# Scan stage of a fused token mixer: projections split 128 + 64, steps reordered, and three of sixteen products with C moved from VectorE to GpSimd

## The chip, the cores and the metric

The kernel runs on one core of a Trainium2 chip. The metric is the device time of one execution in microseconds; three runs of the kernel before gave 1500.68, 1502.33 and 1514.03, median 1502.33. TensorE is PE in the rows, VectorE is DVE, ScalarE is ACT, GpSimd is POOL, the engine that issues most DMAs is SP.

## The reference

Three layers follow each other on 32 sequences of 82 tokens (1 class token, 49 patches, 32 text tokens) of width 192: a convolutional tokenizer, a selective scan (Mamba) block with its gated feed-forward part, and attention with a mixture of experts. The change is in the second one:

```python
h = rmsnorm(x, w_norm1)
z = h @ W_in.T
z = z * sigmoid(h @ W_gate.T)
dt_in, Bm, Cm = split(einsum('bld,kd->blk', z, W_xproj), [96, 112])
dt = softplus(einsum('blr,dr->bld', dt_in, W_dt) + b_dt)
A_bar = exp(dt[..., None] * A)              # A = -exp(A_log), 16 states
Bx = (dt * z)[..., None] * Bm[:, :, None, :]
h_t = A_bar_t * h_(t-1) + Bx_t              # along the tokens
y = einsum('blds,bls->bld', h, Cm) + D_skip * z
x = residual + y @ W_out.T
hf = rmsnorm(x, w_ffn_norm)
out = x + (silu(hf @ W_gate_ffn.T) * (hf @ W_up.T)) @ W_down.T
```

Inner width is 384, the feed-forward width 512. All of it is float32; only the rows of C that TensorE spreads are split into three bfloat16 parts.

## The kernel before

The scan block works in 8 rounds of 4 sequences. N = 328 is the number of tokens of a round, and 384 channels lie on 128 partitions as three blocks, so a full tile of a round is 128x984. The function `mamba` writes each engine's program by hand. A round has 16 steps, one per state s, and `program` (L767) sets for each engine what stands in a step: `step` (the scan of the round i), `post` (output projection and feed-forward of round i-1) and `pre` (norm, z, x-projection, softplus of round i+1). VectorE and GpSimd take `step` first; TensorE and ScalarE take `post` and `pre` first (`side_first`). Round 0 has no post, round 7 no pre.

In a step of the scan:
- GpSimd makes Bx for state s+3 (`inputs`, L1339) from dtz and the rows of B, which SP has spread over 128 partitions through DRAM (Bb).
- ScalarE makes the decays A_bar for state s+2 into two PSUM banks, one per half (`decays`, L1092); each half waits until the scan has read the half before it.
- VectorE multiplies the scanned states hs with C (L1239; called a product here) and then scans the next state in two halves (L1229).
- TensorE spreads the row of C of state s+2 over 128 partitions (L941, `sel`), into one of two banks, waiting for the product that read that bank; then it adds hs times C to y in PSUM by a product with the identity (L956, called y0 to y15 here). After state 15 VectorE drains y (L1195).

Around it, by step: 1 and 2 hold the output projection O in two halves (L905) and the residual adds (L1205), 2 the turn (transpose) of hn (L858), 3 to 5 the three pairs z and gate (L878), each followed by tanh on ScalarE and the z product on VectorE (L1174), 6 the x-projection X (L886), 7 the turn of hf, 8 and 9 the step sizes (L864), 10 to 13 the four pairs of the feed-forward part (L921) with tanh and the av products (L1210, L1213), 14 and 15 the down projection N in two halves (L933). The side work shares two PSUM banks in the order of `SIDE_TILES`; `free` waits until the tile two places before has been read. Softplus is Relu, Abs, Exp (u), two copies that round 1+u (`ax`, L1056 and L1058), Ln (L1060), and four 128x984 operations on GpSimd that end in dt and dtz. The width 192 is contracted as 96 + 96, so a pair of projections is 4 matmuls, and each float32 matmul is 2 passes in the rows.

## Time and profile before

| | us |
|---|---|
| runs | 1500.68, 1502.33, 1514.03 |
| profiled execution | 1509.22 |
| its span | 1507.4 |
| TensorE, VectorE, ScalarE, GpSimd busy in the span | 1240.3, 1035.6, 707.5, 753.8 |
| granted TensorE clock, mean | 0.901 |
| scan rounds 0 to 7 (to the drain of y) | 305 to 833 |

The profiled execution is one run with the hardware profiler on; its rows are in microseconds from the span's start. In a timeline a row stands for instructions of one line that follow each other (x is their number), and the bracket tells how long the engine stood idle before it and what released it. In the windows the last three numbers are the granted clock of TensorE (1.00 is full speed), the DMA share and GB/s.

### The profile page before, as it was taken

To read this page: it belongs to the slowest core of one execution; us is meant where nothing else is said; L and a number is where in the kernel's file an instruction comes from. 1 tells how busy PE (TensorE), PEld (TensorE's weight loads), DVE (VectorE), ACT (ScalarE), POOL (GpSimd) and SP (SyncE) were. 2 spreads that over 40 slices of the span, in tenths; PEclk is the share of its full clock that TensorE was granted. 3 is DMA by queue.
4 is the path that set the end of the run, shared out by engine and by line. 5 is a ranking of instruction groups with operands and counts; after the bars stand their busy time and mean duration, and the time that the engine had idled before them with its cause. 6 is when DMAs were issued, how large, how long until landed. Compare 5 with 4: busy or idle time off the path is not lost. (4 is left out here: it accounts for less than half of the span.)

```text
span 1507.4 us, 19621 instructions
## 1 busy us (share of the span) xinstructions
PE 1240.3 (82%) x5818; PEld 819.3 (54%) x5819; DVE 1035.6 (69%) x1960; ACT 707.5 (47%) x1486; POOL 753.8 (50%) x492
## 2 busy tenths in 40 slices
PE   6796635486989999899987899999996169999996
PEld 4342323242555555555553678877775147777775
DVE  3699787889989899989899556777784313333332
ACT  1137622467868686767765255554531022222221
POOL 2028974378677776858578301144445602222222
PEclk9697657689999999999999899999995579999999
DMA  5100000232404040322310001112211112222221
GB/s 164 54 1 0 28 9 28 99 114 94 135 1 135 0 134 13 121 68 66 131 32 1 1 34 51 45 55 69 61 49 30 37 48 38 35 35 35 38 35 22
DMA packets 71129, 80.89 MB, mean 54 GB/s; under 512 B 13230, under 2 KB 62917, under 8 KB 70969
## 3 DMA queue, kind: packets, MB, share of 16 engines
q1 hardware_dynamic: 51778, 68.50, 14.5%
q0 software_dynamic: 17152, 9.24, 4.5%
q10 hardware_dynamic: 2136, 2.37, 0.6%
q8 instruction: 32, 0.52, 0.2%
q14 instruction: 31, 0.25, 0.1%
HBM read 48.74 MB, written 30.01 MB: 52 GB/s over the span
## 5 line engine op out<-in xcount | busy, mean ns | idle before, releaser
L1346 POOL TENSOR_TENSOR Bx<-dtz,Bb 128x984 f32<-128x984 f32 x128 | 289.1, 2280 | 37.5 <-DVE hs L1229 37.5
L1229 DVE TENSOR_TENSOR_SCAN hs<-ps,Bx 128x492 f32<-128x492 f32 x256 | 287.8, 1165 | 23.2 <-POOL Bx L1346 14.9
L956 PE MATMUL ps<-hs,b_id 128*128 128x492 f32 x512 | 241.0, 593 | 11.9 <-DVE y L1195 9.5
L1100 ACT ACTIVATE ps<-dt,A 128x324 f32<-128x324 f32 (+1 forms) x512 | 212.1, 454 | 78.0 <-DVE hs L1229 77.8
L2070 POOL DMA_INDIRECT out<-yt,dest x48 | 74.2, 1547 | 221.4 <-DVE yt L2057 216.0
L1239 DVE TENSOR_TENSOR hs<-hs,ps 128x984 f32<-128x984 f32 x128 | 150.2, 1173 | 1.9
L1951 PE MATMUL e_ps<-W,xT 97*128 (+1 forms) x384 | 139.2, 505 | 1.6 <-ACT xT L2005 1.0
L956 PEld LDWEIGHTS ps<-hs,b_id 128*128 128x128 f32 x512 | 92.8, 194 | 86.4 <-issue 80.5
L2043 DVE COPY hT__9520<-e_ps 128x768 f32<-128x768 f32 x48 | 46.0, 958 | 131.3 <-PE e_ps L1960 130.9
L1970 PE MATMUL e_ps<-W,hT__9520 128*128 x576 | 109.2, 327 | 0.8 <-DVE yb L2051 0.8
L1846 POOL DMA_INDIRECT buckets<-XS,c_slot x64 | 90.6, 1416 | 37.7 <-DVE c_slot L1808 20.9
L2011 ACT ACTIVATE hb<-e_ps 128x768 f32<-128x768 f32 x48 | 38.9, 811 | 144.9 <-PE e_ps L1951 144.9
L1951 PEld LDWEIGHTS e_ps<-W,xT 97*128 97x128 f32 (+1 forms) x384 | 70.3, 193 | 55.5 <-issue 17.9
L1853 POOL TENSOR_TENSOR c_x<-c_x,bro 82x192 f32<-82x192 f32 x32 | 19.2, 600 | 157.2 <-DVE c_x L1702 157.1
L1970 PEld LDWEIGHTS e_ps<-W,hT__9520 128*128 128x128 f32 x576 | 91.4, 190 | 1.4 <-issue 1.4
L492 POOL TENSOR_TENSOR DF<-DF,prod 96x441 f32<-96x441 f32 x84 | 87.5, 1041 | 6.6
L921 PE MATMUL ps<-hfT,wug 96*128 96x328 f32 x256 | 80.5, 460 | 12.2 <-DVE av L1213 11.5
L1660 DVE TENSOR_REDUCE mx<-ps 82x12 f32<-82x984 f32 x32 | 37.6, 1176 | 59.4 <-PE ps L1565 59.4
L2005 ACT ACTIVATE xT<-e_ps,vec 96x128 f32<-96x128 f32 x96 | 38.5, 451 | 83.8 <-PE e_ps L1941 83.8
L941 PE MATMUL ps<-P,sel 96*128 96x328 bf16 x128 | 39.8, 312 | 45.5 <-DVE hs L1239 32.3
L921 PEld LDWEIGHTS ps<-hfT,wug 96*128 96x128 f32 x256 | 48.3, 196 | 49.8 <-DVE av L1213 27.4
L1578 PEld LDWEIGHTS ps<-V,PT 82*82 82x82 f32 x768 | 65.0, 161 | 11.0 <-issue 4.7
(251 smaller groups left out, 2415.7 us busy)
## 6 DMA issues: line engine op xcount, KB each, us to landing
Bb<-b_rows SPq DMA_DIRECT2D x32, 656.0 KB, 7.0
buckets<-b_zero SPq DMA_DIRECT2D x8, 2288.0 KB, 15.3
xg<-buckets SPq DMA_DIRECT2D x48, 104.0 KB, 1.9
xc<-in_xcol SPq DMA_DIRECT2D x4, 1176.0 KB, 9.2
W<-in_w1d SPq DMA_DIRECT2D x8, 582.0 KB
W<-in_w2d SPq DMA_DIRECT2D x8, 576.0 KB
out<-H SPq DMA_DIRECT2D x8, 246.0 KB
H<-P SPq DMA_DIRECT2D x4, 294.0 KB
```

What stands on the lines that cost most here:

```text
L492: g.tensor_tensor(out, a, prod[:, (9 * n + t) % PRODUCTS], ALU.add).then_inc(s_sum, 1)
L921: mm = pe.matmul(ps[:, wide(name, p), 0:N], wug[:, k, w_, m * 128:(m + 1) * 128], hfT[:, k, :], start=k == 0, stop=k == 1)
L956: mm = pe.matmul(ps[:, BANK_Y + h, 0:HALF], ident[:], f2(hs[:, s % LONG])[:, h * HALF:(h + 1) * HALF], start=s == 0, stop=s == STATE - 1)
L1100: a = act.activation(ps[:, BANK_A + h, c:c + w].rearrange("p (g t) -> p g t", t=S)[:, :, 1:S], dt[:, (par + t // STATE) % 2, m, g0 * S:g1 ...
L1229: v.tensor_tensor_scan(f2(hs[:, t % LONG])[:, c], ps[:, BANK_A + h, 0:HALF], f2(Bx[:, t % RING])[:, c], 0.0, ALU.mult, ALU.add).then_inc(s ...
L1239: v.tensor_tensor(hs[:, s % LONG], hs[:, s % LONG], ps[:, BANK_C + s % 2, 0:N].rearrange("p (a n) -> p a n", a=1).broadcast_to([128, NI, N ...
L1346: g.tensor_tensor(Bx[:, t % RING], dtz[:, p], Bb[:, p, t % STATE, :].rearrange("p (a n) -> p a n", a=1).broadcast_to([128, NI, N]), ALU.mu ...
L1578: mm = pe.matmul(ps[0:S, HEAD_OUT + c % 2, h * (DH + 1):(h + 1) * (DH + 1)], PT[:, c % 2, h, :], V[:, vpar, c, h, :], start=True, stop=True)
L1846: g.indirect_dma_start(out=xs, out_offset=bass.IndirectOffsetOnAxis(ap=slot[:, par, k, c:c + 1], axis=0), in_=XS[:, par, c, :], in_offset= ...
L1951: mm = pe.matmul(ps[:, 1 + 2 * p + h, 0:384], xT[c_, p, k, :], W1[c_, k, bass.ds(e, 1), h * 384:(h + 1) * 384].rearrange("p a n -> p (a n) ...
L1970: mm = pe.matmul(ps[:, 7, 0:D], hT[:, p, k, :], W2[:, k, bass.ds(e, 1), :].rearrange("p a n -> p (a n)"), start=k == 0, stop=k == KF - 1)
L2070: g.indirect_dma_start(out=out, out_offset=bass.IndirectOffsetOnAxis(ap=dest[:, p:p + 1], axis=0), in_=yt[:, p, :], in_offset=None, comput ...
```

## The change

Three things change in `mamba`, and nothing outside it but the layout of its weights.

1. The product with C of states 1, 3 and 5 (`POOLED`) is made by GpSimd from rows of C in SBUF (`Cb`), which SP spreads in one more DMA per round, behind the four of Bb. TensorE spreads 13 rows instead of 16, and adds y of a pooled state together with the next one.
2. The width 192 is contracted as 128 + 64. Of a pair, the two matmuls with 128 rows come first; the two with 64 rows read the lower half of the partitions for one bank and the upper half for the other. The turned hn and hf take 128 partitions, and ScalarE keeps them in three pieces instead of two.
3. The order: O, its residual adds and N are not spread over two steps any more; `dtin` is kept a step later; 1+u is rounded by one two-step operation on GpSimd (on VectorE in the first round) instead of two copies on ScalarE; Ln stands ahead of the second tanh; the relu goes to dt itself; GpSimd waits for u ahead of its Bx 13.

The core of the diff (N is joined in step 14 as O is in step 1, and the residual adds likewise):

```diff
+        POOLED = (1, 3, 5)
+        SPREAD = [s for s in range(STATE) if s not in POOLED]
+        NP_, NS_ = len(POOLED), len(SPREAD)
...
+                sp.wait_ge(s_cst, 2)
+                if j > 0:
+                    sp.wait_ge(s_hp, j * NP_)
+                sp.dma_start(Cb[:], b_d[par, STATE + POOLED[0]:STATE + POOLED[-1] + 1:2, :].rearrange("(a s) n -> a s n", a=1)
+                             .broadcast_to([128, NP_, N])).then_inc(s_Cb, 16)
...
-                        mm = pe.transpose(ps[0:HD, bank(names[k]), q * S:(q + 1) * S], src[:, q, k * HD:(k + 1) * HD],
-                                          ident[0:S, 0:S])
+                        mm = pe.transpose(ps[:, bank(names[k]), q * S:(q + 1) * S], src[:, q, k * 64:k * 64 + 128], ident[0:S, 0:S])
                     mm.then_inc(done, 1)
+
+            def pair(banks, w, x, m, done):
+                c_ = slice(m * 128, (m + 1) * 128)
+                for k in range(2):
+                    pe.matmul(ps[:, banks[k], 0:N], w[:, k, c_], x[:, 0, :], start=True, stop=False)
+                for k in range(2):
+                    half = slice(64 * k, 64 * k + 64)
+                    pe.matmul(ps[:, banks[k], 0:N], w[half, 2, c_], x[half, 1, :], start=False, stop=True).then_inc(done[k], 1)
...
-                    for w_, name, done in ((1, f"RG{m}", s_gt), (0, f"RI{m}", s_zi)):
-                        free(name, j, other)
-                        for k in range(2):
-                            mm = pe.matmul(ps[:, bank(name), 0:N], wzg[:, k, w_, m * 128:(m + 1) * 128], hT[:, k, :],
-                                           start=k == 0, stop=k == 1)
-                        mm.then_inc(done, 1)
+                    free(f"RI{m}", j, other)
+                    pair((bank(f"RG{m}"), bank(f"RI{m}")), wzg, hT, m, (s_gt, s_zi))
...
+                if s == 1:
+                    pe.wait_ge(s_y, p + 1)
+                    for h in range(2):
+                        free(f"O{h}", p, other)
+                        for q in range(2):
+                            c = (2 * h + q) * S
+                            for k in range(NI):
+                                mm = pe.matmul(ps[0:S, bank(f"O{h}"), q * D:(q + 1) * D], y[:, k * N + c:k * N + c + S], wo[:, k, :],
+                                               start=k == 0, stop=k == NI - 1)
+                        mm.then_inc(s_o, 1)
...
-                    for w_, name, done in ((0, f"G{m}", s_g), (1, f"U{m}", s_up)):
+                    if not is_last(p):
+                        free(f"G{m}", p, other)
+                    elif m >= 2:
+                        pe.wait_ge(s_av, p * 4 + (m - 1))
+                    pair((wide(f"G{m}", p), wide(f"U{m}", p)), wug, hfT, m, (s_g, s_up))
...
+            def spread_c(i, par, n):
+                at_least(pe, s_hc, i * NS_ + n - 1)
+                if n % NS_ == 0:
+                    pe.wait_ge(s_P3, i + n // NS_ + 1)
+                pe.matmul(ps[:, BANK_C + (par * NS_ + n) % 2, 0:N], sel[:, SPREAD[n % NS_], :], P3[:, (par + n // NS_) % 2, :],
...
-                if not last or s + 2 < STATE:
-                    spread_c(i, par, s + 2)
+                if s in POOLED:
+                    return
+                n = SPREAD.index(s)
+                if not last or n + 2 < NS_:
+                    spread_c(i, par, n + 2)
+                if s - 1 in POOLED:
+                    add_y(i, s - 1)
                 add_y(i, s)
...
+            def keep_turned(dst, names, v_, done, kept, j):
+                high = slice(64, 128)
+                act.wait_ge(done, j * 2 + 1)
+                act.activation(dst[:, 0, :], ps[:, bank(names[0]), 0:N], ACT.Identity, bias=0.0, scale=vec[:, v_:v_ + 1]).then_inc(kept, 1)
+                act.wait_ge(done, j * 2 + 2)
+                for rows in (high, slice(0, 64)):
+                    a = act.activation(dst[rows, 1, :], ps[high, bank(names[1]), 0:N], ACT.Identity, bias=0.0, scale=vec[high, v_ + 1:v_ + 2])
+                a.then_inc(kept, 1)
...
-                    act.wait_ge(s_u, j + 1)
-                    act.activation(f2(ax[:]), f2(u[:]), ACT.Copy, bias=1.0).then_inc(s_w1, 1)
-                    act.wait_ge(s_w1, j * 2 + 1)
-                    act.activation(f2(ax[:]), f2(ax[:]), ACT.Copy, bias=-1.0).then_inc(s_w1, 1)
-                if s == 11:
-                    act.activation(f2(lnw[:]), f2(u[:]), ACT.Ln, bias=1.0).then_inc(s_c1, 1)
+                if s == 11 and other is None:
+                    logarithm(j)
...
+                    if m == 1 and other is not None:
+                        logarithm(other)
...
+                if s not in POOLED:
+                    n = SPREAD.index(s)
+                    v.wait_ge(s_scan, 2 * (i * STATE + s) + 2)
+                    v.wait_ge(s_pc, i * NS_ + (n + 1))
+                    v.tensor_tensor(hs[:, s % LONG], hs[:, s % LONG],
+                                    ps[:, BANK_C + (par * NS_ + n) % 2, 0:N].rearrange("p (a n) -> p a n", a=1).broadcast_to([128, NI, N]),
+                                    ALU.mult).then_inc(s_hc, 1)
...
-                    g.wait_ge(s_w1, j * 2 + 2)
+                    g.tensor_scalar(f2(ax[:]), f2(u[:]), 1.0, -1.0, ALU.add, ALU.add).then_inc(s_w1, 1)
+                    g.wait_ge(s_w1, j + 1)
                     g.tensor_tensor(f2(ax[:]), f2(u[:]), f2(ax[:]), ALU.subtract).then_inc(s_sp, 1)
                     g.wait_ge(s_sp, j * 2 + 1)
-                    g.tensor_tensor(f2(ax[:]), f2(ax[:]), f2(rl[:]), ALU.add).then_inc(s_sp, 1)
+                    g.tensor_tensor(f2(ax[:]), f2(ax[:]), f2(dt[:, par]), ALU.add).then_inc(s_sp, 1)
...
+            def times_c(i, s):
+                c = POOLED.index(s)
+                if c == 0:
+                    g.wait_ge(s_Cb, i * 16 + 16)
+                g.wait_ge(s_scan, 2 * (i * STATE + s) + 2)
+                g.tensor_tensor(hs[:, s % LONG], hs[:, s % LONG],
+                                Cb[:, c, :].rearrange("p (a n) -> p a n", a=1).broadcast_to([128, NI, N]), ALU.mult).then_inc(s_hp, 1)
+
             def step(i, par, s, last):
+                if s in POOLED:
+                    times_c(i, s)
+                if s == 10 and not last:
+                    g.wait_ge(s_u, i + 2)
```

How it moves the instructions, in a middle round. In the order's rows the register and semaphore instructions are left out. **TensorE**, steps 0 to 4, before (`hs,b_id` is a y, two matmuls each; `P_119,sel` a spread row of C):

```order
L956 MATMUL ps<-hs,b_id 128x492 x2
L905 MATMUL ps<-wo,y 82x192 x6
L941 MATMUL ps<-P_119,sel 128x328
L956 MATMUL ps<-hs,b_id 128x492 x2
L905 MATMUL ps<-wo,y 82x192 x6
L858 MATMUL ps<-b_id,hn 96x82 x4
L858 MATMUL ps<-b_id,hn 96x82 x4
L941 MATMUL ps<-P_119,sel 128x328
L956 MATMUL ps<-hs,b_id 128x492 x2
L878 MATMUL ps<-hT,wzg 128x328 x4
L941 MATMUL ps<-P_119,sel 128x328
L956 MATMUL ps<-hs,b_id 128x492 x2
```

and now:

```order
L968 MATMUL ps<-hs,b_id 128x492 x2
L919 MATMUL ps<-wo,y 82x192 x6
L919 MATMUL ps<-wo,y 82x192 x6
L870 MATMUL ps<-b_id,hn 128x82 x4
L870 MATMUL ps<-b_id,hn 128x82 x4
L950 MATMUL ps<-P_119,sel 128x328
L968 MATMUL ps<-hs,b_id 128x492 x4
L876 MATMUL ps<-hT,wzg 128x328 x2
L879 MATMUL ps<-hT,wzg 128x328 x2
L876 MATMUL ps<-hT,wzg 128x328 x2
L879 MATMUL ps<-hT,wzg 128x328 x2
L950 MATMUL ps<-P_119,sel 128x328
```

Both halves of O stand together, y1 has moved behind the turn to y2, and nothing stands between the first and the second pair.

**GpSimd**, steps 0 to 5 of the same round, now (before, the same rows without those of L1390):

```order
L1375 TENSOR_TENSOR Bx<-dtz,Bb 128x984
L1390 TENSOR_TENSOR hs<-hs,Cb 128x984
L1375 TENSOR_TENSOR Bx<-dtz,Bb 128x984
L1375 TENSOR_TENSOR Bx<-dtz,Bb 128x984
L1390 TENSOR_TENSOR hs<-hs,Cb 128x984
L1375 TENSOR_TENSOR Bx<-dtz,Bb 128x984
L1375 TENSOR_TENSOR Bx<-dtz,Bb 128x984
L1360 TENSOR_TENSOR b_rr<-b_ms,b_nh 82x4
L1390 TENSOR_TENSOR hs<-hs,Cb 128x984
L1375 TENSOR_TENSOR Bx<-dtz,Bb 128x984
```

Each of the three products stands ahead of the Bx of its step and waits for its own scan.

**ScalarE**, step 7, between two steps' decays, now (before, `dtin` stood ahead of the decays, and hfT was two rows of L1085):

```order
L1046 ACTIVATE dtin<-ps 96x328
L1026 ACTIVATE hfT<-ps,vec 128x328
L1029 ACTIVATE hfT<-ps,vec 64x328 x2
L1075 ACTIVATE P_119<-R 32x328
L1076 ACTIVATE Pm<-R 32x328
```

The queue up to the decays for state 9 has `dtin` and one eviction more.

## Rows read from the trace of the kernel before

**Rows 1.** The page's first part: busy us, share of the span, instructions.

```profile
PE 1240.3 (82%) x5818; PEld 819.3 (54%) x5819; DVE 1035.6 (69%) x1960; ACT 707.5 (47%) x1486; POOL 753.8 (50%) x492
```

**Rows 2.** Windows by round: stretch, length, busy PE, PEld, DVE, ACT, POOL, clock, DMA, GB/s.

```profile
502.30:570.90 68.60, 62.72 (x226) 36.56 (x226) 61.78 (x69) 48.20 (x114) 48.62 (x25) 0.98 0.24 74
570.90:637.90 67.00, 61.02 (x226) 35.89 (x226) 61.78 (x68) 48.41 (x115) 48.88 (x25) 1.00 0.24 75
...
775.20:833.40 58.20, 44.54 (x144) 22.57 (x145) 55.70 (x60) 29.58 (x75) 38.95 (x20) 1.00 0.00 1
```

**Rows 3.** VectorE timeline, round from 570.9: start, duration, line, operation [idle before].

```profile
569.73 1.17 DVE L1239 TENSOR_TENSOR hs<-hs,ps 128x984 f32<-128x984 f32 x1
...
581.71 0.52 DVE L1205 TENSOR_TENSOR x<-xl,ps 82x384 f32<-82x384 f32 x1
...
586.89 0.50 DVE L1174 SCALAR_TENSOR_TENSOR z<-sg,ps 128x328 f32<-128x328 f32 x1 [0.36 <-PE ps L878]
587.30 1.17 DVE L1239 TENSOR_TENSOR hs<-hs,ps 128x984 f32<-128x984 f32 x1
588.39 2.25 DVE L1229 TENSOR_TENSOR_SCAN hs<-ps,Bx 128x492 f32<-128x492 f32 x2
...
604.86 2.25 DVE L1229 TENSOR_TENSOR_SCAN hs<-ps,Bx 128x492 f32<-128x492 f32 x2
...
621.38 2.25 DVE L1229 TENSOR_TENSOR_SCAN hs<-ps,Bx 128x492 f32<-128x492 f32 x2 [1.33 <-POOL Bx L1346]
...
628.23 0.50 DVE L1213 SCALAR_TENSOR_TENSOR av<-th,ps 128x328 f32<-128x328 f32 x1
...
637.94 1.61 DVE L1195 SCALAR_TENSOR_TENSOR y<-z,vec,ps 128x328 f32<-128x328 f32 x4
```

**Rows 4.** TensorE timeline of the same round.

```profile
572.70 1.89 PE L956 MATMUL ps<-hs,b_id 128*128 128x492 f32 x4 [1.43 <-DVE y L1195]
574.42 2.11 PE L905 MATMUL ps<-wo,y 128*82 128x192 f32 x12
...
582.29 0.49 PE L858 MATMUL ps<-b_id,hn 82*96 82x82 f32 x4 [1.72 <-DVE x L1205]
...
584.40 2.37 PE L878 MATMUL ps<-hT,wzg 96*128 96x328 f32 x8
...
596.40 3.47 PE L886 MATMUL ps<-z,wx 128*96 128x328 f32 x12
...
628.87 2.80 PE L933 MATMUL ps<-wdn,av 128*82 128x192 f32 x16
```

**Rows 5.** ScalarE timeline of the same round.

```profile
601.99 0.95 ACT L1085 ACTIVATE hfT<-ps,vec 96x328 f32<-96x328 f32 x2
...
612.38 1.01 ACT L1056 ACTIVATE ax<-u 128x984 f32<-128x984 f32 x1
...
616.71 1.28 ACT L1060 ACT_TABLE_LOAD   x1
618.00 1.02 ACT L1060 ACTIVATE lnw<-u 128x984 f32<-128x984 f32 x1
```

**Rows 6.** Windows around the fall of the clock, round from 502.3.

```profile
512.00:514.00 2.00, 0.37 (x5) 0.37 (x6) 2.00 (x4) 0.48 (x1) 0.79 (x1) 1.00 0.00 0
514.00:516.00 2.00, 2.00 (x6) 1.03 (x4) 1.05 (x2) 1.84 (x5) 1.48 (x1) 0.51 0.00 0
```

**Rows 7.** TensorE timeline in the tokenizer: 128-row passes, then 128 and 64 rows.

```profile
99.90 12.02 PE L230 MATMUL ps<-xc,wc 128*128 128x392 f32 x36
...
113.33 0.90 PE L254 MATMUL ps<-D,pwm 128*96 128x392 f32 x2
114.16 0.90 PE L256 MATMUL ps<-D,pwm 64*96 64x392 f32 x2
```

**Rows 8.** GpSimd's groups by shape: count, busy us, mean ns of one.

```profile
L1346 POOL TENSOR_TENSOR Bx<-dtz,Bb 128x984 f32<-128x984 f32 x128 | 289.1, 2280 | 37.5 <-DVE hs L1229 37.5
...
L495 POOL MEMSET PF<- 96x4132 f32 x3 | 10.5, 3539 | 0.1
```

More of the change, by code:

```diff
@@ L79 @@
 V_ROW = 120
-V_N = 121
+V_H_NORM = 121
+V_HF_NORM = 123
+V_N = 125
 CH = 4
@@ L896, in post @@
             def post(p, par, s, other):
-                if s in (1, 2):
-                    h = s - 1
-                    if h == 0:
-                        pe.wait_ge(s_y, p + 1)
-                    free(f"O{h}", p, other)
-                    for q in range(2):
-                        c = (2 * h + q) * S
-                        for k in range(NI):
-                            mm = pe.matmul(ps[0:S, bank(f"O{h}"), q * D:(q + 1) * D], y[:, k * N + c:k * N + c + S], wo[:, k, :],
-                                           start=k == 0, stop=k == NI - 1)
-                    mm.then_inc(s_o, 1)
+                if s == 1:
[8 more added lines that the diff above has]
+                        mm.then_inc(s_o, 1)
                 if s == 7:
@@ L924, in post @@
-                if s in (14, 15):
-                    h = s - 14
-                    if h == 0:
-                        pe.wait_ge(s_av, p * 4 + 4)
-                    if not is_last(p):
-                        free(f"N{h}", p, other)
-                    for q in range(2):
-                        c = (2 * h + q) * S
-                        for k in range(NF):
-                            mm = pe.matmul(ps[0:S, wide(f"N{h}", p), q * D:(q + 1) * D], av[:, k, c:c + S], wdn[:, k, :],
-                                           start=k == 0, stop=k == NF - 1)
-                    mm.then_inc(s_dn, 1)
@@ new lines, in post @@
+                if s == 14:
+                    pe.wait_ge(s_av, p * 4 + 4)
+                    for h in range(2):
+                        if not is_last(p):
+                            free(f"N{h}", p, other)
+                        for q in range(2):
+                            c = (2 * h + q) * S
+                            for k in range(NF):
+                                mm = pe.matmul(ps[0:S, wide(f"N{h}", p), q * D:(q + 1) * D], av[:, k, c:c + S], wdn[:, k, :],
+                                               start=k == 0, stop=k == NF - 1)
+                        mm.then_inc(s_dn, 1)
@@ L978, in ending @@
                 post(last, 1, 1, None)
-                post(last, 1, 2, None)
                 fr.turn(pe)
@@ L1277, in ending @@
                 post(last, 1, 1, None)
-                post(last, 1, 2, None)
                 v.wait_ge(fr.s_r1, 1)
@@ L2082, in _halves, with _two_thirds, _paired @@
     return out
+def _two_thirds(a):
+    import numpy as np
+    a = np.asarray(a).reshape(192)
+    return np.stack([a[0:128], np.concatenate([a[128:192], a[128:192]])], axis=1)
+def _paired(first, second):
+    import numpy as np
+    first, second = np.asarray(first).T, np.asarray(second).T
+    return np.stack([first[0:128], second[0:128], np.concatenate([first[128:192], second[128:192]])], axis=1)
 def _mixed(loc, g):
```

109 lines of the change are left out of this document (50 added, 59 removed).

## The prediction

> **What bounds the kernel now.** The page's totals come first [rows 1]: TensorE 82%, VectorE 69%, GpSimd 50% busy. These are means over stages, so the next view is the windows cut by round of the scan [rows 2]. In a middle round (570.9 to 637.9) TensorE is busy 61.0 us of 67.0, VectorE 61.8, GpSimd 48.9, ScalarE 48.4: two engines are nearly full, the other two have 18 us each. The window 502.3 to 570.9 does the same work in 68.6 us, at a clock of 0.98 instead of 1.00. Four of the six middle rounds are of this kind (68.6 to 68.8 us), two take 67.0. The last round (775.2 on) takes 58.1 and gives TensorE only 44.5 us of work: there VectorE alone sets the pace.
>
> The VectorE timeline of the 67 us round [rows 3] shows two scan halves (2.25 us) and a product with C (1.17; the scan behind it starts after 1.09, 587.30 to 588.39) per state, and where it stands still: 0.36 before the first z, 1.33 before the scan of state 13. The TensorE timeline [rows 4] shows why: after the projections O it waits 1.72 for VectorE's second residual add, and from there to the turn of hf it never stops. So neither engine bounds the round by itself; the chain passes from one to the other, and only what lies on it counts.
>
> **The products on GpSimd.** Three of 16 products per round leave VectorE: 3 x 1.09 = 3.3 us. GpSimd gets them at the price of the Bx row of the same shape, 2.28 us [rows 8], so 6.8 us, and for `ax<-u` a one-source operation of 984 elements: the memset gives a floor of 0.86 ns per element, 0.85 us, the Bx row a ceiling of 2.28. 48.9 + 6.8 + 0.9 to 2.3 = 56.6 to 58.0 us, still under 67. That Bx costs 1.94 times VectorE's product says that the move only pays if GpSimd's time is idle time. The Trainium skill ("GPSIMD Engine Reference", Engine selection) says to keep elementwise work on VectorE, GpSimd being about twice as slow for two inputs. Obeyed, the rule would leave the products where they are; the trace agrees on the price.
>
> **Does the 3.3 us reach the end? A walk through one middle round**, 0 being the start of product 0 (569.73), with durations of rows 3 to 5:
> - Before: second residual add at 12.0 (581.71), first z/gate pair at 14.7 (584.40), z0 at 17.2, projection X at 26.7 (596.40), turn of hf 31.8, scan 9 at 35.1 (604.86), scan 13 at 51.7 (621.38), last av product over at 58.9, next drain at 68.2 (637.94).
> - Now scan 2 follows scan 1 without a product: 5.0 to 7.3. Its decays are just in time (half of the bank is free 1.1 us before, and ScalarE takes 0.85). Then both residual adds stand in one place: y0 from 3.0, O twice 1.95, over at 8.6, so VectorE waits 0.9 us for the second half and does product 2 at 9.1 to 10.2. Of 1.1 saved, 0.9 has become a wait.
> - TensorE stands behind product 2 (C for state 6 first), then adds y1 and y2 together (3.3): pair 0 at 13.75 instead of 14.7, z0 at 16.1 instead of 17.2.
> - Pair 1 needs the bank that z0 frees. Before, y3 covered that wait; now nothing does: TensorE waits 0.6. Pair 1 to 18.8, y3 and y4 to 22.3, pair 2 to 24.5, z2 at 24.6 instead of 25.2.
> - X needs z2, and y5 no longer covers it: X 25.1 to 28.4 (1.6 earlier), but then y5 and y6 stand ahead of the turn of hf: 31.85. Before: 31.8. TensorE's work up to here is the same, so **all of VectorE's 3.3 us has gone into waiting for TensorE**.
> - ScalarE now evicts hf's turn in three pieces instead of two (+0.43) ahead of the decays for scan 9 [rows 5]: scan 9 at 35.5, 0.4 late.
> - Both `ax` copies leave ScalarE (2 x 1.02) and Ln moves ahead of the second tanh. Ln's two table loads and itself (1.28 + 1.02 + 1.28) stay between the decays of states 12 and 13, so VectorE now waits about 0.9 for that tanh where it waited 1.33 for the decays: the 0.4 comes back, scan 13 at 51.7.
> - From the last av product TensorE does N0, N1, y14, y15 in place of N0, y14, N1, y15: the same 9.1 us (628.87 to 637.94). Next drain: 68.2.
>
> Net for a round at full clock: **0 us**, and I allow 1 us either way. GpSimd keeps up: its third product ends near 22.7, Bx 8 at 25 (wanted at 30). The new wait for u ahead of Bx 13 holds Bx 13, the softplus and dtz; by the walk Bx 15 is ready at 58.3 to 59.7 and wanted at 60.1; the two slacks are 5 and at least 0.4. On SP, the rows of C (504 KB) come after the four Bb groups and are used some 35 us later: 0.
>
> **The split 128 + 64.** A pair was 8 passes in 2.21 us, 0.277 each. It stays 8 passes, of which 4 use half the rows. The nearest rows are the tokenizer's [rows 7]: 36 passes of 392 columns with 128 rows take 0.334 each, and where 128 and 64 rows alternate every two passes, 0.415 each. That is 0.16 us per change of height, and a pair has two: +0.33. Against it, two adjacent matmuls on different halves of the array and in different banks may overlap. No row here shows such a pair; between none and both passes that is 0 to -0.55. In the timelines matmuls start in program order, and each is two passes, so only the second pass of the one can lie beside the first of the other: one pass, -0.28. The pair stays at 2.21 + 0.33 - 0.28 = 2.26 (ends 1.98 and 2.54; where drains cost nothing, 1.66). The Trainium skill ("TensorEngine Tiling (Array Packing)", Key Properties) says both that changing the mode drains the array and that tiles run in parallel. By the second alone a pair would take six passes, 1.66; the trace shows the first.
>
> **The clock.** In the 68.6 us rounds the granted clock falls from 1.00 to 0.51, the lower level of 1.2 GHz, right after the 1.72 us pause before the second half of the turn of hn [rows 6, 4], and y2 and the pair behind it run at half speed: 1.6 to 1.8 us a round. By the walk that pause shrinks to 0.2 + 0.7, with 0.6 more at pair 1. I take the drops as gone: **-6.8 us**.
>
> **The other stretches.** Last round: no z, no Ln, TensorE has 14 us to spare, so VectorE's 3.3 less the 0.9 wait come through: **-2.4**. First round: no residual adds, but the same walk (y1 and y2 behind product 2, pair 2 behind y3 and y4) turns the gain into a wait at z2 and leaves -0.3. Ahead of scan 0 VectorE gets one more operation of 984 elements (0 to 1.2, by the product's row), part of it under GpSimd's work: +0.5. After the last round four pairs and one eviction: +0.5. Softplus, table loads, transposes to 128 columns: 0, hidden as before.
>
> **Sum:** 0 - 6.8 - 2.4 - 0.3 + 0.5 + 0.5 = -8.5 on the profiled execution's 1509.2, so 1500.7. That execution is 6.9 us above the median of the three runs (1502.3); on the median: **1494 us**.
>
> **Rivals.**
> - *The clock drops stay* (20%). TensorE still pauses 1.4 us at the drain and several times under 1.1. Against it speaks that the round from 570.9 had the full 1.72 pause and clock 1.00: shorter pauses should bring fewer. Then 1494 + 7 = 1501.
> - *VectorE's time comes through* (20%). If the halves overlap more than I take, or y1 and y2 get out earlier than my walk has them, TensorE gives way at z2 and at hf, where all was lost. At the limit 8 x 3.3 = 26 and the clock's 6.8: 1469; half of it, 1480.
> - *Slower: the change of height, serial.* A pair at 2.54 adds 0.33 at each of seven pairs. Three lie ahead of scan 9 on TensorE's chain, those of states 12 and 13 behind av: about 1.6 to 2.3 a round, +10 to +14 over six, so 1504 to 1508 with the drops gone, 1515 with them. It is slower than before once a pair costs more than about 0.2 net. For it: rows 7; against: the overlap. 15%.
> - *GpSimd late.* The engine that is 1.94 times slower becomes the bound, at Bx 15, whose slack is 0.4 us with the dear one-source operation: 1 us late in six rounds is +6, 1500. For: two new waits in its queue. Against: 9 us idle a round. 5%. The Trainium skill ("GPSIMD Engine Reference", Engine selection) speaks for this one.
> - That the change doesn't move the work is excluded: the order of instructions shows it.
>
> Forecast 40%. **Range 1478 to 1511**: it takes in half of the fast rival, the drops and most of the slow one. The likeliest case's own is 1488 to 1500. Within 1% is 1487 to 1517, about what a measurement can tell. Faster by over 1%: the fast rival and a tenth of the rest, 0.28. Slower by over 1%: the worst of the serial case, 0.08. Within: 0.64.
>
> **What would show it.** Middle rounds all near 67 us, drain to drain, at clock 1.00 (the higher level, 2.4 GHz); VectorE about 58 us busy in each, with new waits at the second residual add (0.9), at z2 (about 2, on TensorE) and before scan 9 (about 2, on ScalarE); the last round near 55.7; pairs near 2.25 us; GpSimd at 57. Wrong, if z2 comes before 24, if pairs leave 2.0 to 2.5, if the clock still drops after the drain, or if scan 15 waits for Bx.

## The result, and the profile after

The changed kernel takes **1528.94 us** (median of 20 runs, 1515.53 to 1536.08), the kernel before 1509.23 (20 runs). The ratio is 1.0116, 95% interval 1.0086 to 1.0146: slower by 1.2%. The forecast was 1494 us, within 1478 to 1511: the kernel was to get faster, and it got slower.

First the page's busy line after (us, share, instructions), to be held against [rows 1]:

```profile
PE 1239.5 (81%) x5794; PEld 798.0 (52%) x5795; DVE 1010.5 (66%) x1938; ACT 700.7 (46%) x1486; POOL 830.7 (54%) x523
```

VectorE has 25 us less, as it should after 24 products. The span went from 1507.4 to 1532.3 all the same. The windows of the changed kernel, cut from drain to drain (length, busy PE, PEld, DVE, ACT, POOL, clock, DMA, GB/s), say where:

```profile
303.90:371.30 67.40, 47.12 (x127) 20.65 (x127) 55.38 (x53) 43.83 (x99) 60.47 (x28) 0.88 0.36 115
371.30:439.60 68.30, 59.87 (x223) 32.02 (x223) 58.18 (x66) 47.83 (x115) 59.29 (x29) 1.00 0.25 83
439.60:509.50 69.90, 60.01 (x224) 32.09 (x224) 58.42 (x66) 48.91 (x116) 60.39 (x29) 1.00 0.25 81
509.50:579.60 70.10, 61.11 (x222) 32.67 (x222) 58.39 (x66) 46.48 (x111) 57.39 (x28) 0.98 0.24 80
...
787.80:846.00 58.20, 44.37 (x140) 21.02 (x141) 52.44 (x57) 29.35 (x76) 47.70 (x24) 0.97 0.08 20
```

Against [rows 2]: a middle round at full clock takes 68.3 us, not 67.0, though VectorE is busy 3.4 us less in it. The first round went from 61.7 to 67.4. The last one gained nothing (58.2). From scan 0 to the last drain the kernel before takes 528.5 us, the changed one 542.2: +13.7, and +13.3 in a second profile of it. Behind the last drain its first profile has 12.2 us more than before. These 12.2 us can't be laid to the change: the second profile of the same kernel has 670.0 us there where the first has 686.3, and before had 674.1. The two windows below are the same 50 us of the span, inside that later stage, in the first profile and in the second (where the stage begins 2.9 us later); the clock is the number behind the busy times:

```profile
1062.60:1112.60 50.00, 47.53 (x343) 39.33 (x343) 30.69 (x95) 21.33 (x40) 22.50 (x19) 0.86 0.21 58
```

```profile
1062.60:1112.60 50.00, 46.71 (x386) 38.91 (x385) 35.67 (x113) 25.18 (x46) 22.83 (x19) 1.00 0.22 62
```

So the loop is read apart from the total below. The medians of 20 runs differ by 19.7 us and the loops of the two profiles by 13.3 to 13.7, so some 6 us of the slowdown lie outside the loop, and no profile here says where. Now one quiet middle round on VectorE (start, duration, line, operation, idle before and its releaser), as in [rows 3]; product 0 is at 438.52:

```profile
438.52 1.17 DVE L1267 TENSOR_TENSOR hs<-hs,ps 128x984 f32<-128x984 f32 x1
...
447.18 0.55 DVE L1231 TENSOR_TENSOR x<-xl,ps 82x384 f32<-82x384 f32 x1 [1.09 <-PE ps L919]
447.65 1.17 DVE L1267 TENSOR_TENSOR hs<-hs,ps 128x984 f32<-128x984 f32 x1
...
454.86 0.50 DVE L1200 SCALAR_TENSOR_TENSOR z<-sg,ps 128x328 f32<-128x328 f32 x1 [1.61 <-ACT sg L1065]
...
463.44 0.49 DVE L1200 SCALAR_TENSOR_TENSOR z<-sg,ps 128x328 f32<-128x328 f32 x1 [2.25 <-ACT sg L1065]
...
474.92 1.18 DVE L1255 TENSOR_TENSOR_SCAN hs<-ps,Bx 128x492 f32<-128x492 f32 x1 [2.79 <-ACT ps L1126]
```

Product 1 took 1.09 us of VectorE's path, and the second residual add now waits 1.09. Then come 1.61 and 2.25 before z0 and z2, and 2.79 before scan 9, which starts 36.4 us into the round (35.1 before). TensorE's side of it, to be held against [rows 4]:

```profile
447.79 0.50 PE L870 MATMUL ps<-b_id,hn 82*128 82x82 f32 x4 [0.36 <-DVE x L1231]
448.88 0.31 PE L950 MATMUL ps<-P,sel 96*128 96x328 bf16 x1 [0.59 <-DVE hs L1267]
449.03 3.47 PE L968 MATMUL ps<-hs,b_id 128*128 128x492 f32 x8
452.33 1.27 PE L876 MATMUL ps<-hT,wzg 128*128 128x328 f32 x4
453.53 0.82 PE L879 MATMUL ps<-hT,wzg 64*128 64x328 f32 x4
455.41 1.37 PE L876 MATMUL ps<-hT,wzg 128*128 128x328 f32 x4 [1.06 <-DVE z L1200]
...
464.08 3.52 PE L901 MATMUL ps<-z,wx 128*96 128x328 f32 x12 [1.15 <-DVE z L1200]
```

y1 and y2 stand together (3.47 us, eight passes) between product 2 and pair 0; y3 and y4 stand so before pair 2. GpSimd's groups in the whole run (count, busy us, mean ns of one, idle before) have two new rows beside [rows 8]:

```profile
L1390 POOL TENSOR_TENSOR hs<-hs,Cb 128x984 f32<-128x984 f32 x24 | 54.5, 2269 | 29.2 <-DVE hs L1255 29.2
L1345 POOL TENSOR_SCALAR ax<-u 128x984 f32<-128x984 f32 x7 | 24.6, 3511 | 0.1
```

### The profile page after: what moved, and what is told of

It is laid out like the page before. It is cut to its first block and busy times, and to the rows that moved or that the text cites. A ratio compares the mean times of both kernels' runs of the same rounds, so it can differ in the third digit from the quotient of the medians.

```text
span 1532.3 us, 19580 instructions
## 1 busy us (share of the span) xinstructions
PE 1239.5 (81%) x5794; PEld 798.0 (52%) x5795; DVE 1010.5 (66%) x1938; ACT 700.7 (46%) x1486; POOL 830.7 (54%) x523
## 5 line engine op out<-in xcount | busy, mean ns | idle before, releaser
L1267 DVE TENSOR_TENSOR hs<-hs,ps 128x984 f32<-128x984 f32 x104 | 122.0, 1173 | 3.8 <-issue 0.9
L1701 DVE TENSOR_REDUCE mx<-ps 82x12 f32<-82x984 f32 x32 | 37.7, 1177 | 66.5 <-PE ps L1606 66.5
L950 PE MATMUL ps<-P,sel 96*128 96x328 bf16 x104 | 32.6, 315 | 55.4 <-DVE hs L1267 43.0
L1390 POOL TENSOR_TENSOR hs<-hs,Cb 128x984 f32<-128x984 f32 x24 | 54.5, 2269 | 29.2 <-DVE hs L1255 29.2
L1606 PE MATMUL ps<-kB,qT 128*82 128x328 f32 (+1 forms) x256 | 65.5, 404 | 3.1 <-DVE E L1705 2.0
## 6 DMA issues: line engine op xcount, KB each, us to landing
buckets<-b_zero SPq DMA_DIRECT2D x8, 2288.0 KB, 16.3
```

Source lines behind the costliest of these rows:

```text
L1267: v.tensor_tensor(hs[:, s % LONG], hs[:, s % LONG], ps[:, BANK_C + (par * NS_ + n) % 2, 0:N].rearrange("p (a n) -> p a n", a=1).broadcast_ ...
L1606: mm = pe.matmul(ps[0:S, SCORES + h0 // 6, (h0 % 6) * S:(h0 % 6 + h1 - h0) * S], qT[:, par, m_, q * S:(q + 1) * S], kB[:, par, m_, q, j:j ...
```

## The experiments

"Loop" is scan 0 to the last drain of the profile, "round" a middle round with full clock and no wait at the loop's end (one round alone in e2, e5, e13 and e16, two in e9, none in e3). Medians are over the runs of each kernel; ratios are to the kernel before on the same chip.

| kernel | median us | ratio (95%) | loop | round |
|---|---|---|---|---|
| before | 1509.2 | 1 | 528.5 | 67.0 |
| changed | 1528.9 | 1.0116 (1.0086 to 1.0146) | 542.2 | 68.3 |
| e1 no products on GpSimd | 1499.95 | 0.9935 (0.9899 to 0.9972) | 511.9 | 64.95 |
| e12 the same again | 1494.5 | 0.9903 (0.9870 to 0.9936) | 511.9 | 64.96 |
| e2 changed, copies on ScalarE | 1527.3 | 1.0141 (1.0089 to 1.0192) | 545.5 | 69.4 |
| e3 before + products only | 1537.7 | 1.0213 (1.0162 to 1.0264) | 555.3 | 71.0 at clock 0.98 |
| e4 changed, again | 1527.1 | 1.0126 (1.0086 to 1.0166) | 541.8 | 68.3 |
| e5 changed, y in turn | 1513.9 | 1.0011 (0.9969 to 1.0052) | 528.4 | 65.4 |
| e6 e1, y in pairs | 1522.9 | 1.0062 (1.0028 to 1.0096) | 538.4 | 68.3 |
| e7 before + order only | 1504.9 | 0.9955 (0.9922 to 0.9988) | 513.1 | 64.9 |
| e8 before + split only | 1517.6 | 1.0039 (0.9997 to 1.0081) | 530.3 | 67.7 |
| e9 products left out | 1491.7 | 0.9903 (0.9868 to 0.9939) | 513.4 | 64.7 |
| e10 e1, copies on ScalarE | 1499.2 | 0.9943 (0.9909 to 0.9976) | 519.9 | 65.9 |
| e11 before + projection in one step | 1490.1 | 0.9875 (0.9827 to 0.9923) | 512.0 | 65.0 |
| e13 e5, counts of 16 | 1511.2 | 0.9996 (0.9954 to 1.0039) | 528.0 | 65.4 |
| e14 e11 again | 1488.2 | 0.9864 (0.9828 to 0.9900) | 512.1 | 65.0 |
| e15 e11, both projections | 1494.7 | 0.9898 (0.9858 to 0.9937) | 511.8 | 65.0 |
| e16 e11 + products, y in turn | 1508.2 | 0.9993 (0.9960 to 1.0026) | 521.5 | 64.9 |

**e1: the change without its products.**

```
- POOLED = (1, 3, 5)
+ POOLED = ()
```

> The changed kernel without its second part: all 16 products with C are on VectorE again, the rows of C are not loaded; the split 128 + 64, the conversion on GpSimd and the order stay. Theory A (the new order and split on TensorE and ScalarE make scans 2, 9 and the residual additions late, whoever multiplies with C): the middle rounds keep 68.0 to 68.6 us (before 66.97, changed 68.35), round 0 gets shorter by 2 to 4, total 1520 to 1530, ratio to the kernel before 1.008 to 1.014. Theory B (GpSimd is too full, its conversion of 3.50 us and three products of 2.27 us make Bx 14 and 15 late): without the three products the waits for Bx go, the middle rounds fall to 67.0 to 67.4 and round 0 to 62 to 63, total 1508 to 1513, ratio 1.000 to 1.003.

The rounds fell below both expectations, to 64.95, each of the six alike and none with a fall of the clock. So the split and the order *gain* 16.6 us in the loop, and the products cost 30, together with the pairs of y: where no state is pooled, no addition is put off to the next step, so this run takes both away and doesn't tell them apart (e5 and e6 do). Neither theory had rounds below 67. Round 0 took 63.8. Such a round in e12's profile (the same kernel), on VectorE, its product 0 at 497.28:

```profile
497.28 1.17 DVE L1260 TENSOR_TENSOR hs<-hs,ps 128x984 f32<-128x984 f32 x1
...
505.44 1.06 DVE L1224 TENSOR_TENSOR x<-xl,ps 82x384 f32<-82x384 f32 x2
506.42 1.17 DVE L1260 TENSOR_TENSOR hs<-hs,ps 128x984 f32<-128x984 f32 x1
...
513.05 0.47 DVE L1193 SCALAR_TENSOR_TENSOR z<-sg,ps 128x328 f32<-128x328 f32 x1
...
520.34 0.47 DVE L1193 SCALAR_TENSOR_TENSOR z<-sg,ps 128x328 f32<-128x328 f32 x1
...
530.32 1.18 DVE L1248 TENSOR_TENSOR_SCAN hs<-ps,Bx 128x492 f32<-128x492 f32 x1 [1.42 <-ACT ps L1119]
```

and on TensorE:

```profile
505.89 1.81 PE L961 MATMUL ps<-hs,b_id 128*128 128x492 f32 x4
507.55 0.73 PE L863 MATMUL ps<-b_id,hn 82*128 82x82 f32 x8
...
509.91 1.27 PE L869 MATMUL ps<-hT,wzg 128*128 128x328 f32 x4
...
521.19 0.99 PE L894 MATMUL ps<-z,wx 128*96 128x328 f32 x3
```

Product 2 starts 9.14 us into the round here and 9.13 in the changed kernel: the product that was taken from VectorE brought it there no earlier. But y1 stands ahead of the turn of hn here, not behind product 2. Nor does TensorE stop once in this round between O and X. In the changed kernel's rows above it waits 0.36, 0.59, 1.06 and 1.15 us there, 3.2 us together, because y1, y3 and y5 no longer fill these places. Pair 0 comes at 12.6 (changed 13.8), z0 at 15.8 (16.3), z2 at 23.1 (24.9), X at 23.9 (25.6) and scan 9 at 33.0 (36.4). The last difference, 3.4, is that of the rounds.

**e2: the copies back on ScalarE.**

```
- g.tensor_scalar(ax, u, 1.0, -1.0, add, add)
+ act.activation(ax, u, Copy, bias=1.0); act.activation(ax, ax, Copy, bias=-1.0)
```

> The changed kernel with the sum and difference of 1 for the softplus made by ScalarE in two copies again, as before, not by one instruction of GpSimd (3.50 us) behind a wait for u ahead of Bx 13. Theory B (GpSimd late through that chain): round 0 falls from 67.4 to 63 to 64, each middle round loses the 0.4 + 0.95 us of waits for Bx (68.35 to 67.2), total 1510 to 1517. Theory A (order and split on TensorE and ScalarE): round 0 gains 3 to 4 us, the middle rounds stay at 68.0 to 68.9 since ScalarE gets two copies more behind which the tanh of the feed-forward gate stands, total 1523 to 1530.

For the middle rounds theory B falls: GpSimd has the 3.5 us less, and the rounds get longer (69.4, against 68.3). VectorE waits 1.81 for the tanh of the second feed-forward quarter where it waited 0.85. Theory A had this total (1527), but rounds of at most 68.9. Round 0 alone gained, 67.4 to 63.3, as both had it.

**e3: the products alone on the kernel before.**

> The kernel before with the second part of the change alone: GpSimd makes products 1, 3 and 5 from rows in SBUF; split 96 + 96, the two copies for the softplus on ScalarE and the order of the rest stay. Theory A: the products by themselves cost nothing; middle rounds 66.6 to 67.1, clock drops of 1.7 us in as many rounds or fewer, total 1500 to 1510, ratio 0.995 to 1.001. Theory B: GpSimd has 6.8 us more in a round, Bx 14 and 15 come 0.5 to 1.5 late and the middle rounds take 67.5 to 68.5, total 1513 to 1521. Third theory (VectorE's 3.3 us come through once the order is the old one): middle rounds 64.5 to 66, total 1490 to 1500.

Worst of all: 71.0 to 73.5 a round, each with a fall of the clock or a wait at the loop's end. The one at full clock takes 71.96 with such a wait of 2.71, so about 69.3 without it. The second residual add is one step later here than in the changed kernel, and in that round z0 waits 2.02, z2 2.48, scan 2 2.04. All three numbers expected were too low.

**e4: the changed kernel again.**

> The changed kernel once more, for a second profile of it. If the 12 us that lie behind the last round are caused by the change, that stretch is again 684 to 688 us; if they are the clock's luck of one execution, it is 672 to 680 with the loop 458 to 463 as before. If the waits of 1.4 us at the loop's branch (two of six rounds) belong to the kernel, they stand in the same rounds again.

Loop 541.8 (first profile 542.2), behind it 670.0 (686.3). The waits at the loop's end stand again in rounds 2 and 4, and the clock falls in rounds 1, 3 and 5. The stretch behind the loop differs by 16 us between two executions of one kernel; the 13.5 us of the loop are the change's.

**e5: y in turn.** `add_y(i, s)` for states 1, 3 and 5 at their own step:

```
  if s in POOLED:
+     add_y(i, s)
      return
...
- if s - 1 in POOLED:
-     add_y(i, s - 1)
```

> The changed kernel with one edit: TensorE adds states 1, 3 and 5 to y each at its own step (behind the output projection, behind pair 0, behind pair 2), not together with states 2, 4 and 6 behind VectorE's next product. In the changed kernel's round from 509.5 product 1 of GpSimd ends at 515.6 and product 3 at 524.9, while TensorE ends the projection at 518.7 and pair 0 at 526.0, so neither is waited for. Theory C (the pairs of additions, 3.5 us in one piece ahead of pairs 0, 2 and the X passes, cost the time): z0 comes 1.65 us earlier, the wait of pair 1 for z0 takes y 3, middle rounds fall from 68.3 (70 with the wait at the loop's end) by 3 to 4 us to 64.5 to 66.5, total 1498 to 1508. Theory D (GpSimd's own work is what costs, as it is slower by twice at the product and then late with Bx): rounds fall by less than 1 us, total 1518 to 1530.

Quiet rounds fall from 68.3 to 65.4, the loop by 13.8 us. The total lies at 1514, 6 above the expected range, since the waits at the loop's end and the clock drops stayed. Theory C holds for the rounds, D falls.

**e6: the same edit the other way.** In e1, with all products on VectorE:

```
+ if s in (1, 3, 5): return
+ if s in (2, 4, 6): add_y(i, s - 1)
  add_y(i, s)
```

> The kernel of the run without products on GpSimd (1499.95 us, rounds of 64.95) with one edit the other way: all 16 products on VectorE, but TensorE adds states 1 and 2, 3 and 4, 5 and 6 to y in pairs, behind product 2, 4 and 6, as in the changed kernel. Theory C: the round gets longer by most of what the changed kernel loses, 2 to 4 us (67 to 69), total 1512 to 1525. Theory D: 0 to 0.8 us a round, total 1498 to 1506. If VectorE being ahead is needed for the loss as well (it has 3.3 us less in the changed kernel), something between, with z0 late by 1.65 and no more.

64.95 becomes 68.32, the changed kernel's round, with GpSimd doing no product at all. VectorE's waits are those of the changed kernel:

```profile
458.51 0.50 DVE L1195 SCALAR_TENSOR_TENSOR z<-sg,ps 128x328 f32<-128x328 f32 x1 [0.49 <-ACT sg L1060]
467.10 0.49 DVE L1195 SCALAR_TENSOR_TENSOR z<-sg,ps 128x328 f32<-128x328 f32 x1 [1.20 <-ACT sg L1060]
478.57 1.18 DVE L1250 TENSOR_TENSOR_SCAN hs<-ps,Bx 128x492 f32<-128x492 f32 x1 [2.88 <-ACT ps L1121]
```

They are shorter at z0 and z2 by what VectorE itself now has to do, and nearly the same at scan 9 (2.88, 2.79). This pair of runs, e5 and e6, shows it from both sides: the placing of three additions on TensorE costs 2.9 us a round with GpSimd's products and 3.4 without them. Round 0 gets 4.7 us longer by it as well (68.5 against 63.8).

**e7 and e8: the order alone, the split alone, on the kernel before.**

> The kernel before with the order of the change alone (both halves of the output projection and of the residual additions in one step, both halves of the last projection in one step, the logarithm and the copy of dt_in later on ScalarE, the conversion on GpSimd), split 96 + 96, all products on VectorE. The two parts together brought the middle rounds from 66.97 or 68.65 to 64.95. If the order brings it: rounds of 65 to 66 and no clock drops, total 1500 to 1505. If the split brings it: rounds of 67 to 68.6, total 1507 to 1513.

> The kernel before with the split 128 + 64 alone, its order as before. The pair takes 2.02 us from start to end and not 2.21 + 0.33 twice over: three pairs in the first half of a round and four in the second make TensorE's part shorter by 0.5 each, 3.5 us a round. If the split brings the 2 us (and the end of the clock drops): rounds of 65 to 66, total 1500 to 1505. If the order brings it: 67 to 68.6, total 1506 to 1513. Evictions of the turned rows take 1.66 instead of 0.98 us, so a loss of up to 0.7 is possible too.

The order brings it all (64.9; the clock falls in one middle round, which takes 66.5, where it fell in four before). The split alone loses 0.7 a round (67.7): the turned rows leave in three evictions, the tanh waits for the whole pair, and VectorE waits 1.65 and 2.08 for decays behind them. Its 1518 us lie above both ranges. With the new order the same split costs nothing that the rounds show (64.95 against 64.9).

**e9: products left out.** Nobody multiplies states 1, 3 and 5.

> Leaves out part of the computation: nobody multiplies states 1, 3 and 5 with C (the output is not the reference's). Otherwise the kernel with y in turn, and no rows of C in SBUF, so VectorE is relieved of 3 x 1.09 us a round and GpSimd has nothing more to do. Theory E (in states 0 to 8 the chain from the drain over projection, residual additions, pairs and evictions on TensorE and ScalarE sets the pace, so VectorE's relief is worth nothing there): rounds of 64.5 to 65.4, as with all products on VectorE (64.95), total 1498 to 1508. If VectorE's time counted and GpSimd's slower product (2.27 us, rows of C, order behind Bx) ate it up: rounds of 62 to 63.5, total 1480 to 1492. The waits of 0.5 to 1.15 us without a releaser at the end of every second round: if they come from VectorE's shorter program they stand here too (total then 1501 to 1512), if from GpSimd's products they are gone.

Theory E holds for the rounds: 64.7, only 0.25 less than with all products on VectorE. The total, 1491.7, lies below its range, but e12 on the same chip has 1494.5 and the same ratio, 0.9903. One window of a quiet round, and, from another round, two of the waits that took the 3.3 us:

```profile
696.50:761.20 64.70, 59.22 (x223) 31.82 (x223) 58.33 (x67) 47.03 (x112) 52.24 (x26) 1.00 0.31 96
```

```profile
571.30 0.55 DVE L1223 TENSOR_TENSOR x<-xl,ps 82x384 f32<-82x384 f32 x1 [1.09 <-PE ps L912]
...
575.94 1.18 DVE L1247 TENSOR_TENSOR_SCAN hs<-ps,Bx 128x492 f32<-128x492 f32 x1 [0.83 <-ACT ps L1118]
```

VectorE waits for TensorE's projection, then for ScalarE's decays. Against e5 (65.4), GpSimd's slower products cost 0.7 a round. The waits at the loop's end stand here too, so they do not come from GpSimd's products.

**e10: e1 with the copies on ScalarE.**

> The kernel without products on GpSimd (1499.95 us) with the sum and difference of 1 again as two copies on ScalarE in place of one conversion on GpSimd of 3.50 us. If GpSimd's 3.5 us and its wait for u are what makes Bx 15 late by 1.1 us a round: the wait goes and rounds fall to 64.0 to 64.4, total 1492 to 1497. If ScalarE's two copies (1.9 us together, ahead of the first tanh of the feed-forward part) delay as much: 64.9 to 66.5, total 1499 to 1508.

The second: scan 15 no longer waits for Bx, but the tanh comes 2.21 late, and the round takes 65.9. Round 0 is the other way, 60.9 against 63.8, since there Bx 15 waits 3.3 us for the conversion. The conversion on GpSimd is worth 1 us a middle round and costs 2.9 in the first.

**e11 and e14: one piece of the order.** The kernel before with this alone, on TensorE and in the same way for the adds on VectorE:

```
- if s in (1, 2):
-     h = s - 1
+ if s == 1:
+     for h in range(2):
```

> The kernel before with one piece of the new order: both halves of the output projection in one step of TensorE and both residual additions in one step of VectorE. TensorE's 24 passes then stand in one piece and x1 is complete one step (about 3.9 us) earlier, and the turn of hn, pair 0 and z 0 stand as before. If this piece brings the order's 2 us: rounds of 65 to 66, total 1500 to 1506. If the last projection in one step, the later logarithm and dt_in and the conversion bring it: 66.6 to 68.6, total 1506 to 1512.

> The kernel before with both halves of the output projection and of the residual additions in one step, once more (four runs that count gave 1490.12 us, ratio 0.9875). Rounds of 65.0 again; expected 1490 to 1500 us and a ratio of 0.988 to 0.994, about that of the split and order together without products (0.9903 and 0.9935).

65.0 a round, loop 512.0 and 512.1: this piece is the order's whole gain. One middle round (66.7) still has a fall of the clock. The ratios are the lowest of all (0.9875 and 0.9864, the second just below what was expected), though their intervals overlap those of e9 and e12. Its TensorE rows, to be held against 572.70 to 582.29 of [rows 4], and the residual adds on VectorE:

```profile
566.38 4.06 PE L904 MATMUL ps<-wo,y 128*82 128x192 f32 x24
...
572.08 0.73 PE L858 MATMUL ps<-b_id,hn 82*96 82x82 f32 x8
```

```profile
569.97 1.06 DVE L1202 TENSOR_TENSOR x<-xl,ps 82x384 f32<-82x384 f32 x2
```

Both turns of hn run in one piece. The pause of 1.72 us between them is gone, and with it the pauses of 0.95, 0.36, 0.25 and 0.24 us that VectorE made in that part of the round before, 1.8 us of the 1.95.

**e12: e1 again.**

> The split and the order of the change with all products on VectorE once more, beside the run with the copies. The first time it took 1499.95 us, ratio 0.9935. Expected again 1498 to 1502 us, rounds of 64.95; if the first result was the chip's, the ratio lies above 0.998.

Loop 511.9 again. Its median is 4 us over e11's, which ran on the same chip, with an equal loop. The difference lies outside the loop, where single executions differ by up to 16 us, and I can't lay it to an edit.

**e13: counts of 16.**

```
- .then_inc(s_pc, 1)
+ .then_inc(s_pc, GAP[n % NS_])
```

`GAP` is 2 where a state is skipped, 1 elsewhere, so the count runs to 16 a round instead of 13; the count of VectorE's products (`s_hc`) is changed likewise.

> The kernel with y in turn (1513.88 us), with the semaphores of the C rows and of VectorE's products counting 16 a round in place of 13 (an increment of 2 where a state is skipped); no engine does other work. VectorE's loop body is then 263 instructions long, not 287 (269 in the kernel before). If the length of that body causes the 1.4 to 1.8 us of waits without a releaser at the end of rounds 2 and 4, they go and the ten further instruction transfers (41 against 31) with them, total 1509 to 1512. If the waits come from another thing in the kernels with 13 products, they stay, total 1513 to 1515.

The waits at the loop's end stand, although the total, 1511.2, falls into the range of the theory that they go:

```profile
504.53 1.18 DVE L1268 TENSOR_TENSOR hs<-hs,ps 128x984 f32<-128x984 f32 x1 [0.38 <-issue]
506.78 1.61 DVE L1223 SCALAR_TENSOR_TENSOR y<-z,vec,ps 128x328 f32<-128x328 f32 x4 [1.07 <-issue]
```

So do the 41 transfers on the instruction queue q14 (31 in every kernel with 16 products on VectorE, 41 or 42 in every one with 13). The lengths in the expectation leave out the instructions that only wait for a semaphore or signal one. With them the trace has 343 instructions of VectorE in two rounds (one pass of the loop's body) before, 331 in the changed kernel and 331 in e13. So this edit left the length as it was, and length is not excluded: every kernel with these waits has 331, every one without them 343, give or take a record. What the trace adds is where the ten further transfers lie. Six of them follow the two branches back to the loop's start, three behind each, of 8 KB. In the changed kernel the branch starts at 504.27 and VectorE's next instruction 2.86 us later, against 0.35 us before (500.60 to 500.95). The instruction queue in the changed kernel's window 504 to 511:

```profile
q14 instruction: 3, 0.02, 1.1%
```

The kernel before has none on that queue in 490 to 790. That the waits are waits for instructions is the likely reading; no run tests it, nor whether the length of the body or its place in VectorE's program brings the transfers on.

**e15: the last projection in one step too.**

> As the kernel with the output projection's halves in one step, and the 32 passes of the feed-forward's last projection in one step too. There VectorE waited 0.52 us a round for the second half of it: that wait goes, and the wait of 1.33 us for ScalarE or Bx at scan 14 or 15 takes some of it. Rounds of 64.5 to 65.0, total 0 to 4 us below the kernel with the first piece alone. A loss of up to 0.5 a round if y 14, now behind all 32 passes, makes the drain wait.

No gain: the rounds stay at 65.0, and the 0.52 before the second half becomes 0.67 before the drain.

**e16: the products on the best order.**

> Best case for the products on GpSimd: the kernel before with the output projection's halves in one step, products 1, 3 and 5 on GpSimd, y in turn, counts of 16. Theory E (the chain on TensorE and ScalarE sets the first half of a round): rounds of 65.0 to 65.8, not shorter than the 65.0 without products, and total 1497 to 1506. If the relief of VectorE is worth something on this order: rounds of 62 to 64.3, total 1480 to 1490.

The quiet round takes 64.9 against 65.0. The loop is 9.4 us longer by the waits at the loop's end, a single one up to 2.7 us here, and the clock drops behind them; the total, 1508, lies 2 above theory E's range.

## Why the prediction was wrong

**The walk through the round had the right places and too small waits.** It gave 9.1 for product 2 (measured 9.13), 13.75 for pair 0 (13.8), 16.1 for z0 (16.3), 24.6 for z2 (24.9), 25.1 for X (25.6), 31.85 for the turn of hf (32.4), 35.5 for scan 9 (36.4). The tanh came 0.85 behind, as said. Each small error has one sign. I let the gate's half of a pair end before the pair; in the rows both end together, so the tanh and z0 come later and pair 1 waits 1.06, not 0.6. The three evictions took 1.66 us where two took 0.98: +0.68, not +0.43. Scan 9 was 1.3 late, not 0.4: 0.6 from the turn of hf, 0.7 from the evictions.

**The step that failed is "the 0.4 comes back ... Net for a round at full clock: 0".** What is late at scan 9 does not come back: e1 to the changed kernel, scan 9 moves by 3.4 and the round by 3.4; before to changed, by 1.3 and 1.4. From scan 9 on VectorE is the pace, and a wait for the tanh only takes the place of a wait for the decays. Six rounds of 1.4 are 8 us. Two of the prediction's own signs of being wrong came with it: scan 15 waits for Bx (0.95), and the clock still falls behind the drain.

**"All of VectorE's 3.3 us has gone into waiting for TensorE" was right and half the truth.** e9 shows that the relief is worth 0.25 us on this order (e16 against e11: 0.1). But I set the time by comparing with the kernel before and so added two large effects to a nought without seeing either: the projection in one step gains 2 us a round (e11), the pairs of y lose 3 (e5, e6). I had written down both, "both residual adds stand in one place" and "adds y1 and y2 together (3.3)", and priced neither by itself.

**The first round** was to gain 0.3 and lost 4.4 to 5.7. Of it, 2.1 belong to the rest of the change (e1: 63.8 against 61.7). There Bx 15 comes 3.3 late behind the conversion, with no product on GpSimd. The remaining 2.3 to 3.6 come with the products and the pairs of y; the pairs by themselves add 4.7 (e6), the products without the pairs 2.0 (e5).

**The one-source operation** took 3.50 us, outside my bounds of 0.85 to 2.28. I had taken a memset for its floor and an operation with two inputs for its ceiling. GpSimd is busy 59.3, 60.4 and 57.4 us in the three middle rounds shown, not 57, and scan 15 waits 0.95 for Bx. In the middle rounds it is a miss of the size and not the cause of the loss: with the two copies on ScalarE in its place they got longer (e2 by 1.1, e10 by 1.0). In the first round it costs 2.9 (e10). The Trainium skill ("GPSIMD Engine Reference", Engine selection) calls work with one input on GpSimd "roughly line-rate"; this row disagrees, since VectorE did the same operation in 0.73 us.

**The split:** a pair takes 2.02 us from start to end (452.33 to the end at 454.35), of which four passes of 64 rows take 0.82. I had 2.26 with ends at 1.98 and 2.54, and before it was 2.21. The change of height and the overlap together come out 0.2 us shorter; what each is worth by itself no row tells (both at their best would be my 1.66). The rival of the serial pair falls all the same, as it needs 2.54. The kernel was slower by another mechanism.

**The clock, -6.8:** only half came. Two of the four drops went; two stayed, in rounds 3 and 5 (in e4's profile three, the third in round 1). Each stands behind a wait at the loop's end that I had no term for, 1.4 us in the changed kernel. The windows from 511 on show it (clock behind the busy times), at the lower of the two levels, 1.2 GHz:

```profile
511.00:513.00 2.00, 1.73 (x3) 0.95 (x4) 2.00 (x3) 0.74 (x2) 0.00 (x0) 0.69 0.00 0
513.00:515.00 2.00, 2.00 (x5) 0.94 (x4) 1.98 (x3) 1.43 (x4) 1.63 (x1) 0.50 0.00 0
```

Ahead of it VectorE stood still twice with nothing that releases it, and TensorE waited 2.35 us for the drain:

```profile
507.37 1.18 DVE L1267 TENSOR_TENSOR hs<-hs,ps 128x984 f32<-128x984 f32 x1 [0.46 <-issue]
509.51 1.61 DVE L1222 SCALAR_TENSOR_TENSOR y<-z,vec,ps 128x328 f32<-128x328 f32 x4 [0.96 <-issue]
```

**The last round** was to gain 2.4 and gained 0 (58.2) or 1.0 (57.2 in e4). e9, with the products gone, has 55.8 against e1's 58.3, so 2.5 us were there to be had. GpSimd's products eat much of it up, though not everywhere (e3, on the old order, has 56.3): with y in turn (e5, 60.3) TensorE has little else to do, waits 2.54 and 2.31 us for two of them, and runs at the lower clock behind each wait. Here, unlike in the middle rounds, GpSimd's own slowness shows:

```profile
791.00 2.92 PE L968 MATMUL ps<-hs,b_id 128*128 128x492 f32 x4 [2.54 <-POOL hs L1389]
```

The middle rounds add up: 6 x 1.4 = 8.2 longer, 2 waits of 1.55 at the loop's end, 2 drops of 1.7 against 4 before: 8.2 + 3.1 - 3.4 = 7.9. With 5.7 for the first round and 0.1 for the last it is the loop's 13.7. The forecast had -9.5 for the loop, so 23 of the 35 us between forecast and measurement lie there.

**The base:** 6.9 us more come from the last step of the sum, which took the profiled execution to be 6.9 above the median. Three runs gave 1502.3; the median of 20 is 1509.2, the profiled execution itself. The other 5 us lie outside the loop and are not explained.

## What to carry to other kernels

Where an engine's work is made by two others in turn, give each result its own place in the consumer's queue: here three additions batched behind the next product cost 3 us a round, while the work that was moved was worth 0.25. Price an order and the work moved along with it one by one, each against the same base; a sum of nought between two versions can be +2 and -3. Before relieving an engine, leave the work out altogether once: that bounds what a better place for it can bring on that order.

## What the hardware showed

- GpSimd's operation with one input and two scalar steps on 128 x 984 elements takes 3.50 us, longer than its product of two inputs (2.27).
- Matmuls of 64 rows on the two halves of the array, in different banks, take less time than those of 128 rows: four passes of 328 columns in 0.82 us where four of 128 rows take 1.2. As 64 rows alone were no faster beside 128 in the tokenizer [rows 7], this points to overlap of the halves. The alternation in the tokenizer, 0.415 a pass [rows 7], was no guide to it.
- All kernels with 13 products on VectorE, and none with 16, have waits of 1.2 to 3.2 us in all without a releaser at the end of the loop's body, and 41 or 42 transfers on the instruction queue instead of 31, three of 8 KB behind each branch back. With the products the length of the body changes too (331 instructions against 343), and its place in the program, so which of these brings them on is open.
- The stretch behind the loop takes 670 to 687 us in the profiles, 16 us apart in two profiles of one kernel. Comparisons of less than that need the loop apart.
